# Routing moved into the attention steps of a gated cross-attention block with a mixture of experts

## Chip, cores and metric

The kernel runs on one core of a Trainium2 chip. The metric is the device time of one execution in microseconds (us). Three timed runs of the kernel before are 759.17, 760.97 and 762.27 us; their median is 760.97.

## The reference, cut to what matters

There are 64 sequences of 64 tokens with 128 features (4096 tokens), in float32. All learned scales and biases are drawn at random, so none can be left out.

```python
x = x + tanh(g_xattn) * cross_attention(layernorm(x), ctx)   # 16 heads of 64, q and k layer-normed per head, softmax, Wu, bu
h = layernorm(x)
probs = softmax(h @ Wg)                        # 8 experts
vals, idx = top_k(probs, 2); weights = vals / (sum(vals) + 1e-9)
routed = sum over the two chosen e of weights[e] * (silu(h @ W1[e] + b1[e]) @ W2[e] + b2[e])   # 128 -> 512 -> 128
shared = silu(h @ Ws1 + bs1) @ Ws2 + bs2
x = x + tanh(g_ffn) * (routed + 0.1 * shared)
```

## The kernel before

The tokens are 32 tiles of 128 (two sequences each). Every engine has its own queue, run in the order in which the code is written; semaphores carry the dependences. PE is the matmul engine, DVE, ACT and POOL are the vector, scalar and GpSimd engines, SP issues DMAs. Large projections are made of three float32r passes on a high and a low part of each operand: ACT copies the high part, POOL or DVE subtracts it from the value for the low part.

**Attention.** A Python loop over steps s writes out, for each engine, what it does for a tile and its neighbours: projections of q and k for tiles s+1 and s+2, normalisation, transposes, scores of tile s, softmax (DVE maxima and subtraction, ACT exponential, DVE row sums and reciprocals, then POOL's `normalise_rows`, one multiplication over 128x1024), the attention output of tile s-1 and the output projection of tile s-2. The calls in each engine's `step(s)` are its order. In the same steps ACT and POOL split a 160-column slice of the expert weights W1 (`expert_weights`). At s == 1 ACT issues the loads of all expert weights (`load_experts`).

**Routing and shared expert.** After attention, `groups` runs over eight groups of four tiles; groups 0, 1, 6 and 7 are written out, the others are a loop. A group computes the shared expert's hidden layer and result for group g, logits for group g+1, and the choice of experts for g: softmax over 8, `max` and `max_index` per tile, one-hot masks, running counts in bfloat16, and a matmul with a triangular matrix that gives each token its rank. POOL then scatters the normalised rows into the `routed` table in device memory, one region for each expert, one indirect DMA per tile and choice. DVE adds the shared result to the residual (`shared_out`). At the end DVE makes a schedule of 39 row tiles of 256 rows, and the ends of regions are filled with padding rows.

**Routed tiles.** For each of the 39 tiles SP loads 256 rows (four buffers), PE transposes them, ACT and DVE split them, DVE copies the W1 parts of the expert, PE does hidden layer and result, and POOL scatters the result by the row's index (`xs_ix`) into `results`. The last stage reads both results of each token and adds them with their weights.

Of the kernel before, what the change touches and what calls it, by code (L numbers as in the profile page):

```python
# [13 lines left out]
P = 128  # L14
# [9 lines left out]
GT = 4  # L24
# [3 lines left out]
ROW = D + 1  # L28
# [10 lines left out]
def flamingo_block(nc, x, xT, ctxT, g_xattn, g_ffn, wqT, wkT, wvT, wuT, bu, qn_w, qn_b, kn_w, kn_b,  # L39
                   wg, w1, b1, w2, b2, ws1, bs1, ws2, bs2, out):  # L40

    with ExitStack() as stack:
# [15 lines left out]
        xc_hi = sb("xc_hi", [P, 2, 2, P], F32R)  # L58
        xc_lo = sb("xc_lo", [P, 2, 2, P], F32R)
# [17 lines left out]
        spo = sb("spo", [P, 2 * E * (D + 1)])  # L77
# [14 lines left out]
        mv = sb("mv", [P, 2, 2])  # L92
# [5 lines left out]
        w1_raw = sb("w1_raw", [P, NX, FF])  # L98
# [8 lines left out]
        rows = late[:, 0:2 * 2 * GT * ROW].rearrange("p (u c j n) -> p u c j n", u=2, c=2, j=GT)  # L107
        o = 2 * 2 * GT * ROW
        router = {}
        for name, width in (("lg", GT * E), ("gm", GT), ("gs", GT), ("gtop", GT * 8), ("gidf", GT * 2), ("gw", GT * 2),  # L110
                            ("oh", 2 * GT * E), ("rank", GT * E), ("hit", 2 * GT * E), ("slotf", 2 * GT)):
            router[name] = late[:, o:o + width]
            o += width
        assert o <= 3 * INNER
        gp = router["lg"].rearrange("p (j e) -> p j e", j=GT)
        gm, gs = router["gm"], router["gs"]
        gtop = router["gtop"].rearrange("p (j e) -> p j e", j=GT)
        gidf = router["gidf"].rearrange("p (j e) -> p j e", j=GT)
        gw = router["gw"].rearrange("p (j e) -> p j e", j=GT)
        oh = router["oh"].rearrange("p (c j e) -> p c j e", c=2, j=GT)  # L120
        rank = router["rank"].rearrange("p (j e) -> p j e", j=GT)
        hit = router["hit"].rearrange("p (c j e) -> p c j e", c=2, j=GT)
        slotf = router["slotf"].rearrange("p (c j) -> p c j", c=2)
        y8 = prob[:, 0:4, :, :].rearrange("p a b n -> p (a b n)")
        spare_hi, spare_lo = (w[:, :, :].rearrange("p a n -> p (a n)") for w in (w_hi, w_lo))
        gT = spare_lo[:, 0:2 * GN].rearrange("p (u n) -> p u n", u=2)
        gT_hi, gT_lo = gT[:, 0, :], gT[:, 1, :]
        act = wide[:, 0:2, :].rearrange("p a n -> p (a n)").rearrange("p (c n) -> p c n", c=CH)
# [4 lines left out]
        normed = wide[:, 2:4, :].rearrange("p a (j n) -> p a j n", n=D)[:, :, 0:GT, :]  # L133
        gidx = sb("gidx", [P, GT, 8], U32)
        chosen = sb("chosen", [P, 2, GT, E], BF16)
# [86 lines left out]
        def steps(step):  # L222
            for s in range(-5, TILES + 5):
                step(s)
# [1043 lines left out]
```

## Time and profile before

| | us |
|---|---|
| median of three runs | 760.97 |
| profiled execution, own time | 757.15 |
| its span, first to last instruction | 755.1 |
| PE busy | 612.6 (81%) |
| DVE busy | 480.6 (64%) |
| ACT busy | 456.8 (60%) |
| POOL busy | 363.6 (48%) |

The profile is of one execution; the time around its span is 2.05 us. A matmul in float32 shows as two instructions. Busy times overlap between engines; a queue named with a q (ACTq, SPq) is the time an engine spends on issuing a DMA or on registers. "issue" and "remote" name idle time whose cause the profile does not show.

### The profile page before, as it was taken

Reading aid. Unit: us, or ns where it says so; the run is one execution under the profiler, and the core shown is the slowest. Engines: PE = TensorE matmul, PEld = TensorE weight load, DVE = VectorE, ACT = ScalarE, POOL = GpSimd, SP = SyncE. Lnnn points to the kernel's source line nnn. Section 1 sums busy time; section 2 is a strip of 40 time slices with the busy share of each in tenths; the row PEclk is TensorE's granted clock in tenths of the full one; section 3 lists DMA queues with packets and bytes.
Section 4 is the critical chain, followed back from the end, with each engine's and each line's share of the span. In section 5 each row is a group of like instructions: output and inputs, shape, how many; then the busy total and the mean of one; then the engine's idle time right before and its main releaser. Section 6 shows DMA issues by size and latency. Waiting matters only on the chain.

```text
span 755.1 us, 21530 instructions
## 1 busy us (share of the span) xinstructions
PE 612.6 (81%) x7702; PEld 531.3 (70%) x7702; DVE 480.6 (64%) x1191; ACT 456.8 (60%) x967; POOL 363.6 (48%) x713
## 2 busy tenths in 40 slices
PE   3709999999999999999998588777734989898950
PEld 1508787877878778787787476766634989898940
DVE  5626888888888888888887356645552444444417
ACT  4517888888888888888887235333402545454515
POOL 3423556555555555555654315554461545454540
PEclk9869999999999999999999668887865999999985
DMA  7180000000100000000000040111033212222218
GB/s 245 41 263 18 2 30 3 3 30 2 31 2 3 30 3 30 2 3 3 2 2 3 1 79 32 40 35 35 29 79 63 76 59 76 67 72 71 72 42 327
DMA packets 30038, 37.90 MB, mean 50 GB/s; under 512 B 4993, under 2 KB 20625, under 8 KB 29809
## 3 DMA queue, kind: packets, MB, share of 16 engines
q1 hardware_dynamic: 20800, 21.42, 9.5%
q0 software_dynamic: 4720, 9.89, 4.0%
q10 hardware_dynamic: 4416, 5.25, 2.6%
q8 instruction: 62, 1.02, 0.6%
q14 instruction: 40, 0.32, 0.1%
HBM read 23.13 MB, written 13.42 MB: 48 GB/s over the span
## 4 chain that ended last, share of the span: by engine, by line
PE 56%; ACT 11%; DVE 11%; issue 8%; another core or an unknown queue 5%; DMA 3%; ACTq 3%; POOL 2%; SPq 0%; DVEq 0%; POOLq 0%
PE ps L1039 8%; PE ps L1221 8%; PE ps L1012 6%; PE ps L1014 5%; PE ps L1013 5%; PE ps L1065 4%; PE ps L1048 4%; ACT prob L419 4%; PE ps L1080 4%; PE ps L1207 3%; PE ps L1209 3%; ACT qk_T L404 3%; PE ps L1208 2%; ACTq L348 2%
## 5 line engine op out<-in xcount | busy, mean ns | idle before, releaser
L663 POOL DMA_INDIRECT results<-spo,xs_ix x78 | 75.2, 964 | 87.2 <-DVE spo L986 72.2
L740 DVE TENSOR_REDUCE ss<-wide 128x16 f32<-128x1024 f32 x64 | 78.1, 1220 | 53.0 <-ACT wide L380 45.9
L509 ACT ACTIVATE qk_T<-ps,b_cols 128x256 f32<-128x256 f32 x156 | 61.9, 474 | 75.9 <-PE ps L1209 69.9
L404 ACT ACTIVATE qk_T<-ps,lnw 128x512 f32<-128x512 f32 x128 | 96.7, 787 | 15.4 <-issue 14.1
L1039 PE MATMUL ps<-ident,wide 128*128 128x128 f32 x512 | 76.3, 282 | 32.3 <-ACT qk_T L404 31.5
L1039 PEld LDWEIGHTS ps<-ident,wide 128*128 128x128 f32 x512 | 57.9, 142 | 58.8 <-ACT qk_T L404 44.5
L1012 PE MATMUL ps<-w_hi,xc_hi 128*128 128x512 f32 x192 | 91.7, 477 | 7.3 <-DVE w_lo L683 3.8
L646 POOL DMA_INDIRECT routed<-w_raw,slot x64 | 62.2, 972 | 70.9 <-issue 53.3
L747 DVE TENSOR_TENSOR wide<-ps,rstd 128x512 f32<-128x512 f32 x128 | 81.7, 680 | 3.7 <-POOL rstd L598 3.3
L380 ACT ACTIVATE wide<-ps 128x512 f32<-128x512 f32 x128 | 77.3, 606 | 5.0 <-PE ps L1014 5.0
L1014 PE MATMUL ps<-w_hi,xc_lo 128*128 128x512 f32 x192 | 77.2, 402 | 0.0
L1013 PE MATMUL ps<-w_lo,xc_hi 128*128 128x512 f32 x192 | 76.9, 401 | 0.0
L1221 PE MATMUL ps<-w_sb,qk_T 128*128 x624 | 76.9, 277 | 0.0
L1221 PEld LDWEIGHTS ps<-w_sb,qk_T 128*128 128x128 f32 x624 | 73.8, 194 | 0.0
L1094 PEld LDWEIGHTS ps<-wu_sb,spo 128*128 128x128 f32 x512 | 63.5, 196 | 5.3 <-ACT spo L434 2.8
L1094 PE MATMUL ps<-wu_sb,spo 128*128 128x128 f32 x512 | 64.2, 280 | 2.5 <-ACT spo L434 2.5
L604 POOL TENSOR_TENSOR prob<-prob,rinv 128x1024 f32<-128x1024 f32 x32 | 61.0, 1905 | 9.2 <-DVE rinv L776 9.2
L1207 PE MATMUL ps<-w_lo,w_hi 128*128 128x256 f32 x156 | 49.0, 314 | 8.5 <-DVE w_lo L957 8.4
L769 DVE TENSOR_REDUCE sm<-prob 128x16 f32<-128x1024 f32 x32 | 39.1, 1221 | 17.5 <-ACT prob L419 17.5
L755 DVE TENSOR_REDUCE mx<-ps 128x8 f32<-128x512 f32 x64 | 41.2, 686 | 12.5 <-PE ps L1065 12.4
L957 DVE TENSOR_TENSOR w_lo<-ps,w_lo 128x256 fp32r<-128x256 f32 x39 | 16.6, 425 | 49.3 <-ACT w_lo L500 38.8
L1012 PEld LDWEIGHTS ps<-w_hi,xc_hi 128*128 128x128 f32 x192 | 37.2, 194 | 15.2 <-DVE w_lo L683 5.8
(175 smaller groups left out, 1419.7 us busy)
## 6 DMA issues: line engine op xcount, KB each, us to landing
v_sb<-routed SPq DMA_DIRECT2D x39, 129.0 KB
xc_in<-in_x SPq DMA_DIRECT2D x8, 256.0 KB, 2.9
xc_in<-in_ctx SPq DMA_DIRECT2D x8, 256.0 KB, 3.2
w_raw<-in_L_ffn_W ACTq DMA_DIRECT2D x1, 2048.0 KB, 9.7
wide<-results SPq DMA_DIRECT2D x4, 512.0 KB, 4.9
w_raw<-results SPq DMA_DIRECT2D x4, 512.0 KB, 8.0
out_x<-x_res SPq DMA_DIRECT2D x8, 256.0 KB, 3.9
x_res<-in_x SPq DMA_DIRECT2D x1, 1792.0 KB, 8.5
```

The lines of the kernel that those rows point to most:

```text
L380: nc.scalar.activation(sq[:, n, j * 512:j * 512 + 512], ps[2 * n + j][:, :], ACT.Square, scale=HD ** -0.5).then_inc(sq_ready[n][j], 1)
L404: nc.scalar.activation(qk_T[:, n, 4 * j:4 * j + 4, :].rearrange("p a n -> p (a n)"), ps[6 + j][:, :], ACT.Identity, bias=lnw[:, 2 * n + 1: ...
L663: gp_.indirect_dma_start(out=results[:, :], out_offset=bass.IndirectOffsetOnAxis(ap=xs_ix[:, b4, a:a + 1], axis=0), in_=yb[:, b4, a, :], i ...
L740: nc.vector.tensor_reduce(ss[:, n, :], sq[:, n, :].rearrange("p (h d) -> p h d", h=HEADS), AX.X, ALU.add).then_inc(ss_ready[n], 1)
L747: nc.vector.tensor_tensor(qk_n[:, n, j * 512:(j + 1) * 512].rearrange("p (h d) -> p h d", h=8), ps[2 * n + j][:, :].rearrange("p (h d) -> ...
L1012: nc.tensor.matmul(out_bank, xc_hi[:, t % 2, src, :], w_hi[:, w, cols[j]], start=True, stop=False)
L1013: nc.tensor.matmul(out_bank, xc_hi[:, t % 2, src, :], w_lo[:, w, cols[j]], start=False, stop=False)
L1014: return nc.tensor.matmul(out_bank, xc_lo[:, t % 2, src, :], w_hi[:, w, cols[j]], start=False, stop=True)
L1039: last = nc.tensor.transpose(ps[6 + j][:, a * P:(a + 1) * P], qk_n[:, n, c0:c0 + P], ident[:, :])
L1094: last = nc.tensor.matmul(ps[7][:, 0:D], o_T[:, p, :, :].rearrange("p b n -> p (b n)"), wu_sb[:, p, :], start=(p == 0), stop=(p == PAIRS - 1))
L1207: nc.tensor.matmul(h, w_hi_c, xs_hi[:, n % 2, :], start=True, stop=False)
L1221: last_ = nc.tensor.matmul(ps[4 + n % 2][:, a * D:(a + 1) * D], hT[:, n % 2, c, a * P:(a + 1) * P], w2e[:, c, :], start=(c == 0), stop=(c ...
```

## The change

- Routing is worked into the attention steps. Tile s-3 is normalised, transposed and multiplied by Wg (float32, no split) inside step s. The choice is made for batches of eight tiles, in eight pieces, one per step from step 12 on (`batch_at`, `route`), straight behind the row reciprocals on DVE. It finds the best expert by maximum, equality and a factor that prefers the first of ties, and then the second; counts are per batch. The last of the four batches is done after attention.
- The scatters are two per step from step 20 on POOL (`SCATTER_LAG`); the rest follow the steps. Rows are scattered from one table `rows_all` of all tiles; both choices send the same row, which carries the token's index and its first expert, so that the reader can tell first from second choice.
- Order within `step` is new on all engines; token parts have four buffers in place of two (`XD`). POOL splits W1's low part (the rest) a step after ACT's high part. W1 is handled in 27 parts of 176 or 160 columns.
- Expert loads are issued by SP, W1 one expert at a time into two buffers. The bias loads and all padding writes are on SP too; DVE makes the padding in place of POOL.
- The shared expert is written out, with two buffers for its inputs, activations and sums; its first two hidden layers stand among the last attention steps.
- Rows have 130 columns, and the 256 rows of a routed tile lie two per partition.

```diff
 def step(s):                                   # PE
-    project_qk(0, 1, s + 1)
-    transpose_qk(0, 1, s, before_q)
-    project_v(1, s)
...
-    transpose_probabilities(0, s - 1, before_p)
-    transpose_probabilities(1, s - 1, before_p)
-    scores(s)
-    attend(s - 1)
+    if s == TILES:
+        transpose_tokens(0)
+        transpose_tokens(1)
+        shared_hidden(0)
+    transpose_probabilities(0, s - 1, before_p)
+    transpose_probabilities(1, s - 1, before_p)
+    scores(s)
+    attend(s - 1)
+    project_qk(0, 1, s + 2)
+    transpose_qk(0, 0, s + 1, before_q)
+    logits(s - 4)
+    route_ranks(s, 12)
+    transpose_qk(0, 1, s + 1, before_q)
+    project_qk(1, 1, s + 2)
+    project_v(0, s + 1)
+    transpose_normed(s - 3)
+    project_out(s - 1)
+    transpose_qk(1, 0, s + 1, before_k)
+    project_qk(1, 0, s + 2)
+    transpose_qk(1, 1, s + 1, before_k)
+    project_v(1, s + 1)
+    project_qk(0, 0, s + 3)
+    if s == TILES:
+        transpose_tokens(2)
+    if s == TILES + 1:
+        shared_hidden(1)
 def step(s):                                   # DVE
+    sum_squares(0, s + 1)
+    scale(1, 0, s)
+    row_sums(s - 1)
+    row_inverses(s - 1)
+    route(s, 12)
     residual(s - 2)
-    token_statistics(s + 3)
     scale(0, 0, s + 1)
-    scale(0, 1, s + 1)
     sum_squares(1, s + 1)
+    scale(0, 1, s + 1)
+    normalise(s - 3)
+    token_statistics(s + 3)
     second_statistics(s - 2)
     maximum(1, s)
     maximum(0, s)
     less_maximum_of(1, s)
+    scale(1, 1, s + 1)
     less_maximum_of(0, s)
-    sum_squares(0, s + 2)
-    scale(1, 1, s + 1)
-    scale(1, 0, s + 1)
-    row_sums(s)
-    row_inverses(s)
+    route_ranks(s, 12)
+    keep_logits(s - 4)
 def step(s):                                   # POOL
+    scatter(s - SCATTER_LAG)
+    variance(1, s)
+    newton_step(1, s)
+    output_bias(s - 2)
+    token_eps(s + 1)
+    expert_weights(s - 1)
+    low_part(s + 3)
+    second_rstd(s - 3)
+    variance(0, s + 1)
+    newton_step(0, s + 1)
+    normalise_rows(s - 1)
+def route(s, lag):                             # DVE, one piece per step
+    b, at = batch_at(s, lag)
...
+    if at == 0:
+        less_highest(b)
+    if at == 1:
+        expert_probabilities(b)
+        highest(0, gp)
+        ties(0, gp)
+    if at == 2:
+        chosen(0)
+        without_first()
+        highest(1, rest)
+    if at == 3:
+        ties(1, rest)
+        chosen(1)
+    if at == 4:
+        count(b)
+    if at == 5:
+        fill_ranks(b)
+        name_first(b)
+    if at == 6:
+        place(b)
+    if at == 7:
+        weigh(b)
+def scatter(t):                                # POOL
+    if has(t):
+        gp_.wait_ge(f_slot, t // BT + 1)
+        for c in range(2):
+            gp_.indirect_dma_start(out=routed[:, :], out_offset=bass.IndirectOffsetOnAxis(ap=slot[:, t // BT, c, t % BT:t % BT + 1], axis=0),
+                                   in_=rows_all[:, t, :], in_offset=None).then_inc(f_sent, 16)
 # PE, after the steps
+shared_result(0)
+for g in range(1, GROUPS):
+    if g + 2 < GROUPS:
+        transpose_tokens(g + 2)
+    if g + 1 < GROUPS:
+        shared_hidden(g + 1)
+    if g == 1:
+        ranks(NB - 1)
+    shared_result(g)
 # routed tiles
-sp.dma_start(xs_in[:, b4, :, :], routed[bass.ds(row, RT), :].rearrange("(a p) n -> p a n", p=P)).then_inc(r_in[b4], 16)
+sp.dma_start(xs_in[:, b4, :, :], routed[bass.ds(row, RT), :].rearrange("(p a) n -> p a n", p=P)).then_inc(r_in[b4], 16)
-nc.vector.tensor_copy(xs_ix[:, b4, :], xs_in[:, b4, :, D].bitcast(I32)).then_inc(r_ix, 1)
+nc.vector.scalar_tensor_tensor(xs_ix[:, b4, :], xs_in[:, b4, :, D + 1], sched[:, 0, n:n + 1], xs_in[:, b4, :, D],
+                               ALU.not_equal, ALU.add).then_inc(r_ix, 1)
```

On DVE, the order after the steps is: the last batch's choice with `lo_part(2)` in it, `shared_out(0)`, `lo_part(3)`, the last slots, `make_padding`, `shared_out(1)`, `lo_part(4)`, the schedule of 22 short linked instructions, and then the other sums and low parts.

## Rows read from the trace of the kernel before

**Rows 1.** Stretches: length, busy (count) PE PEld DVE ACT POOL, clock, DMA share, GB/s.
```profile
61.30:412.40 351.10, 334.81 (x5567) 278.26 (x5566) 287.63 (x501) 298.62 (x620) 198.20 (x496) 1.00 0.03 10
440.60:577.80 137.20, 91.33 (x561) 79.81 (x560) 74.94 (x393) 44.78 (x63) 62.20 (x64) 0.76 0.19 46
577.80:735.00 157.20, 142.62 (x1168) 139.93 (x1166) 64.34 (x190) 72.38 (x194) 75.20 (x78) 0.97 0.21 65
```

**Rows 2.** Chain that ended last: start us, us, what (L1065 is the scores).
```profile
61.34 1.09 PE ps L1065 x64
...
391.75 1.09 PE ps L1065 x64
...
412.47 1.14 PE ps L1065 x64
...
429.82 0.36 DVE x_res L723
...
569.31 3.86 DMA routed<-w_raw,slot
```

**Rows 3.** Timeline of ACT at start-up: start us, us, what, idle before.
```profile
42.28 12.17 ACTq L348 DMA_DIRECT2D w_sb<-in_L_ffn_Ws  x1
...
55.46 0.78 ACT L404 ACTIVATE qk_T<-ps,lnw 128x512 f32<-128x512 f32 x1 [14.11 <-issue]
```

**Rows 4.** Timeline inside an attention step, PE and POOL.
```profile
199.93 1.09 PE L1039 MATMUL ps<-ident,wide 128*128 128x128 f32 x8 [0.48 <-ACT qk_T L404]
...
200.36 1.91 POOL L604 TENSOR_TENSOR prob<-prob,rinv 128x1024 f32<-128x1024 f32 x1
```

**Rows 5.** Groups by line, 440 to 560 us: busy us, mean ns, idle before.
```profile
L646 POOL DMA_INDIRECT routed<-w_raw,slot x56 | 54.5, 973 | 65.1 <-issue 47.5 <-DVE slot L913 17.6
...
L873 DVE TENSOR_TENSOR w_raw<-iot,w_raw 128x32 f32<-128x32 f32 x16 | 2.3, 191 | 0.0
...
L911 DVE TENSOR_REDUCE w_raw<-w_raw 128x8 f32<-128x64 f32 x8 | 1.8, 220 | 0.3
```

**Rows 6.** Lines L804 and L683: ns minimum/median/maximum, first and last start us.
```profile
L804 DVE TENSOR_SCALAR wide<-x_res,mv,rstd x32: 328/346/3556, 430.6 to 522.0; 128x128 f32<-128x128 f32 x16, 128x128 f32 x16
...
L683 DVE TENSOR_TENSOR w_lo<-w_raw,w_hi x4: 692/693/860, 10.2 to 15.7; 128x512 fp32r<-128x512 f32 x4
```

**Rows 7.** Timeline at start-up, POOL and DVE.
```profile
16.15 2.57 POOL L621 TENSOR_TENSOR w_lo<-w_raw,w_hi 128x512 fp32r<-128x512 f32 x2 [4.46 <-ACT w_hi L373]
...
16.27 1.30 DVE L780 TENSOR_SCALAR tgbu<-bu_b,tg 128x128 f32<-128x128 f32 x1
```

**Rows 8.** Timeline after attention, POOL's padding fill.
```profile
432.04 1.82 POOL L650 MEMSET spo<- 128x2064 f32 x1
```

**Rows 9.** Timeline from the last scatters to the first routed tile.
```profile
555.79 0.96 POOL L646 DMA_INDIRECT routed<-w_raw,slot  x1 [0.30 <-issue]
...
559.54 0.17 DVE L931 CAST cnt_i<-run 128x8 int32<-128x8 f32 x1
...
565.15 0.20 DVE L952 CAST sched_i<-sched 128x78 int32<-128x78 f32 x1
...
567.16 0.43 DVE L971 CAST w_hi<-w_hi 128x512 fp32r x1 [0.42 <-issue]
...
577.84 0.58 PE L1207 MATMUL ps<-w_lo,w_hi 128*128 128x256 f32 x1
```

**Rows 10.** Timeline of PE in group 1: hidden layer, transposes, result.
```profile
452.29 0.48 PE L1156 MATMUL ps<-w_lo,w_hi 128*128 128x512 f32 x1
...
455.19 0.60 PE L1141 MATMUL ps<-ident,wide 128*128 128x128 f32 x4
...
456.81 3.81 PE L1168 MATMUL ps<-w_sb,wide 128*128 128x128 f32 x32 [1.03 <-ACT wide L480]
```

**Rows 11.** Waits in total, 440 to 560 us: us, times, longest us.
```profile
ACT w_raw L475 <- DVE w_raw L842: 68.8, 8, 9.9
POOL routed L646 <- issue: 47.5, 55, 5.8
```

More of the change, by code:

```diff
@@ L254, in eps_of, with batch_at @@
             return eps_q[:, t % 4:t % 4 + 1] if n == 0 else eps[:, 1, 0:1]
[L256 to L264 removed]
+        def batch_at(s, lag):
+            b, at = divmod(s - lag, BT)
+            return (b, at) if 0 <= b < NB - 1 else (None, 0)
         def r_slot(n):
@@ new lines, in _ @@
+            load_expert(0)
+            load_expert(1)
+            load_experts()
+            for s in range(TILES):
+                c, at = divmod(s, CK)
+                if at == 0 and c + 2 < TILES // CK:
+                    sp.wait_ge(xlo_ready, CK * (c + 1))
+                    load_tokens(c + 2)
+                e, part = divmod(s - W1_FIRST, len(W1_PARTS))
+                if part == len(W1_PARTS) - 1 and 2 <= e + 2 < NX:
+                    load_expert(e + 2)
+            sp.dma_start(b1_cols[:, :], b1).then_inc(bias_in, 16)
@@ L466, in _ @@
+                if s == TILES:
+                    shared_silu(0)
             steps(step)
[L468 to L483 removed]
@@ L485, in _ @@
[L485 to L494 removed]
+            hi_part(2)
+            expert_exponentials(NB - 1)
@@ new lines, in route_ranks, with transpose_tokens @@
+            def route_ranks(s, lag):
+                b, at = batch_at(s, lag)
+                if b is not None and at == RANKS_AT:
+                    ranks(b)
+            def transpose_tokens(g):
+                pe.wait_ge(norm_ready, GT * g + GT)
+                if g == 0:
+                    pe.wait_ge(sub_ready[0], TILES)
+                else:
+                    pe.wait_ge(f_lo, g)
+                for j in range(GT):
+                    last = nc.tensor.transpose(ps[4][:, j * P:(j + 1) * P], rows_all[:, GT * g + j, 0:D], ident[:, :])
+                last.then_inc(f_t, 1)
@@ new lines, in shared_result @@
+            def shared_result(g):
+                pe.wait_ge(act_ready, CH * (g + 1))
+                if g >= 1:
+                    pe.wait_ge(f_x2, 2 * g - 1)
+                else:
+                    pe.wait_ge(o_ready[0], TILES)
+                for j in range(GT):
+                    for c in range(CH):
+                        last = nc.tensor.matmul(ps[6][:, j * D:(j + 1) * D], act[:, g % 2, c, j * P:(j + 1) * P], w2_sb[:, E, c, :],
+                                                start=(c == 0), stop=(c == CH - 1))
+                last.then_inc(fy_done, 1)
```

651 lines of the change are left out of this document (325 added, 326 removed).

## Prediction, made before the changed kernel was run

> **What bounds the kernel now.** I read the table of stretches first, cut where the work changes [rows 1]. Up to 61.3 us is start-up. From 61.3 to 412.4 us the attention steps run: PE is busy 334.8 of 351.1 us at full clock, DVE 287.6, ACT 298.6, POOL 198.2. The score matmuls in the chain give the period: from 61.34 (token tile 1) to 391.75 (tile 29) is 28 periods of 11.80 us [rows 2]. Per step that is PE 11.25 busy and 0.55 idle, DVE 9.67, ACT 10.04, POOL 6.66. So PE bounds a step, with only 0.55 us in which it stands. From 440.6 to 577.8 us the routing and the shared expert take 137.2 us, of which PE is busy 91.3 at clock 0.76 and no engine is full: this stage is a ring of waits. From 577.8 us the 39 routed tiles run, PE busy 142.6 of 157.2; then the last sums. The change aims at the third stage and pays in the second.
>
> **Start-up.** The old load_experts sat on ACT's queue. The issue for the small Ws2 load took 12.17 us there, because the large W2 load ahead of it had to be taken in first, and ACT's next operation came after 14.11 us of idleness [rows 3]. In the new kernel these loads are on SP, where only loads needed several steps later stand behind them; W1 comes expert by expert. W1's two first parts are ahead of W2, and tokens for tiles 8 on are first needed at step 4. I take the whole 14.1, and 1.0 more because PE came back at the lower clock. **-15.** If SP's loads came late instead, the cover would be gone and up to all 15 lost.
>
> **The attention steps, PE.** Per tile a transpose of the normalised rows and a logits matmul are added, each two passes. A transpose pass is one 128-column instruction that PE issues every 0.14 us (1.09 us for eight [rows 4]); so 0.27 for the transpose, and, as its weight load is the same, 0.25 for the logits. Two rank matmuls per eight tiles are under 0.1. Sum 0.52 on 11.25: 11.8 if all gaps close, 12.3 if the present 0.55 stays. The order is rewritten so that each projection stands between a copy and the matmul that needs it; I take 12.1, thus +0.3 a step. For the eleven periods before routing starts (score tiles 1 to 12): **+3**.
>
> **The attention steps, DVE.** From step 12 each step carries an eighth of a batch's choice. The pieces have 34 instructions for 8 tiles, most of 64 elements. The nearest rows are 0.22 us for a reduction over 64 and 0.19 for a two-input operation on 32 [rows 5], and the wait on DVE's own last instruction adds about 0.02: 34 times 0.21 is 7.1 us per batch, 0.9 a step. The normalising of a tile is 0.33 (the minimum in [rows 6]) and the logits copy 0.17. That makes 9.67 + 0.9 + 0.33 + 0.17 = 11.1 us, still under PE.
>
> But the piece stands straight behind the reciprocal of the row sums, and that is what releases POOL's 1.9 us multiplication over the probabilities [rows 4]. What such a pair does is seen at start-up: the 128x128 tensor_scalar that takes 0.33 elsewhere took 1.30 when it began at 16.27, 0.12 us after POOL began the first of its two 1.28 us subtractions; of 32 normalisations one took 3.56 us, while POOL cleared the padding; and a two-input subtraction with both inputs in SBUF took 0.86 against 0.69 when a POOL subtraction was under way [rows 6 to 8]. So an operation that needs both SBUF inputs can be held until POOL is done. All eight pieces contain two-input operations on SBUF; the first short instruction slips in, the rest would stand up to 1.7 us. Bounds: 0 and 1.7 a step; I take 1.5, since each of the three shows a hold where POOL overlapped, though the last only a part of it. Then DVE needs 12.6 a step, and in its fixed order nothing else can fill the hole: residual, two scalings, a reduction, two statistics stand behind the piece, and PE's next score-dependent work waits for the maxima behind those. I take 12.7, 0.9 over the present, for the 17 periods from tile 12 to tile 29: +15.3. The last two periods are now 20.7 us together [rows 2] and bound by latency; I take 23 for them. **+18** together.
>
> The Trainium skill, page "SBUF — State Buffer", section "Who interferes with whom", says that a DVE instruction with two SBUF inputs and a GpSimd instruction that reads SBUF exclude each other for the whole instruction, and that a reduction never does. By that rule the hold is about 1.8 us and the period 12.9 to 13.0, 4 us more in all; without any hold it would be 12.1, 10 us less. The long tensor_scalar rows agree with it in kind [rows 6, 7]; the 0.86 us row is shorter than a full hold.
>
> **ACT and POOL in the steps.** ACT gains a 128x128 copy, some 0.3, and one exponential in eight: 10.4 of 12.1. Its W1 piece is 176 wide, not 160. POOL gains from step 20 two scatters per step, each 0.97 busy [rows 5] and, at its closest, 0.30 apart [rows 9]: 2.5, so 9.2 of 12.7. Ahead of the reciprocal roots on POOL's queue they delay the key scaling; that scaling is needed only after the next scores and POOL has 3.5 us to spare, so nothing. The single-tile expert loads are covered by three steps of lead, and SP's waits for POOL's subtraction hold up only loads that are wanted later.
>
> **From the last scores to the routed tiles.** Now: 412.47 to 577.84, 165.4 us [rows 2, 9]. The last tile's residual begins 17.3 us after its scores began [rows 2]; attend and output ran at the low clock there. In the new kernel the shared expert's first hidden layers are put among them, so PE stays busy; at the upper clock this piece loses about 3, giving 14.5. Statistics, root, normalising, transpose, copy, logits and copy for tile 31 are seven short links of 0.2 to 0.6, about 3.5. So the choice for the last eight tiles can start 18 us after the last scores began.
>
> After that, PE has eight shared results, six hidden layers, five sets of four transposes. A hidden layer took 2.9 us at full clock (452.29 until 455.2) and a result 3.6 (the 3.81 row less the overlap of its last matmul) [rows 10]; transposes 0.6: 28.8 + 17.4 + 3.0 = 49.2. DVE meanwhile has the last choice (34 x 0.21 = 7.1), the padding it takes from POOL (a fill of 2064 columns is 1.82 us on POOL [rows 8]; I take that and 1.6 for the shorter one on DVE too), the schedule (559.54 to 565.35, 5.8 us [rows 9]) and the sums of each group (1.4 and 0.7). Since result g waits for sum g-1, PE stands about 2, 1 and 1.2 us behind these three lumps: 4.4. That replaces the ring that now costs about 15 us per group: there ACT waits 68.8 us in eight waits for the logits' maximum [rows 11], and the exponential, hidden activations and result stand in series behind. Scatters: 32 of them are left, 1.26 each, 40 us, plus 3.9 us to the last landing [rows 2]; their last slots are ready 12 us after the choice starts. They end near 43 of the 54 us: hidden, with 11 us to spare. The eight padding transfers on SP start once the counts are known, some 15 us into this phase, and have the rest of it.
>
> Then the last sum (1.4), DVE's four W1 copies of 0.43 with 0.4 before each pair [rows 9] (2.5) and the first low part (0.4): 4.3 us. Total 18 + 49.2 + 4.4 + 4.3 = 76, against 165.4: **-89.5**.
>
> **Routed tiles.** Rows of 520 B, two per partition, halve the packets of the loads, but PE is the bound there at 91% of the stretch, and the loads wait in four buffers: 0. The index operation now compares the expert, 0.05 more on a DVE busy 64 of 157 us: 0. At the beginning PE ran at the low clock until about 582; after dense work it need not: **-2**.
>
> Sum: -15 + 3 + 18 - 89.5 - 2 = -85.5. The profiled execution has 757.15 us of its own, 2 over its span, and lies 3.8 under the median of 760.97. So 671.7 in its terms, 675.5 in those of the median: I say **674**.
>
> **Rivals.** (a) No hold, PE bounds all steps. For it: DVE's tiny inputs may not need the port for long. Against: [rows 7]. Step 11.85 to 12.1: total 652 to 664. Chance 0.22. The forecast itself, steps of 12.4 to 13.2, has 0.5 and its own range 664 to 688.
> (b) The shared expert stays stop-and-go: PE falls to the low clock (it is 0.76 there now [rows 1]) or each result waits for a sum; then a group costs 9.5 instead of 7.1, over seven groups +17, total about 691. Against: its inputs are ready one group ahead. Chance 0.16.
> (c) The gain is cut because scatters, not PE, release the routed tiles: at 2.0 us each rather than 1.26, 24 us more, less 11 to spare: 687. For: they share POOL and DMA with padding; against: the 56 of now have a mean of 0.97 [rows 5]. Chance 0.08.
> (d) Slower: POOL's queue. If a scatter inside a step waits as long as its longest idle gap now (5.8 us, the longest of 55 [rows 11]), POOL gets past the reciprocal roots late, scaling follows and every step with scatters grows. It decides from 85.5/16 = 5.3 us a step; at 5.8 on top of the forecast it gives 674 + 93 = 767. Against: slots are written a step or more before. Chance 0.02. The last 0.02 is for about no change.
>
> **Numbers.** From (a) through (b): 652 to 696 leaves out about 2 in 10 at the two ends. What a measurement here can tell from no change is about 0.5%, 3.8 us. Faster 0.96, within 0.02, slower 0.02.
>
> **What would show it.** Score matmuls of neighbouring tiles 12.1 apart up to tile 12 and 12.7 beyond it; in heavy steps a two-input DVE instruction of the piece 1 to 1.8 us long, ending with POOL's multiplication; no idle of 14 us in ACT; PE's gap before the first routed matmul under 5 us; the shared phase near 7.1 us per group at a clock near 1. Wrong it would be above all if the heavy steps are far from 12.7, or if long instruction waits turn up in the code of the groups, which is now written out.

## The result: 714.6 us, faster, but by 47 us and not by 87

The changed kernel took 714.63 us (median of four runs, 712.04 to 716.72) beside 761.43 for the kernel before: a ratio of 0.9371, 95% interval 0.9333 to 0.9408. Faster, as predicted, but outside the range of 652 to 696. The profiled execution took 712.84 us, its span is 710.8.

One thing has to be said before any number below is read. The experiments ran in five batches on chips of the same kind, each batch beside the kernel before. In two batches the kernel before took 712.8 and 712.5 us, in three 750.5, 762.2 and 760.5, and the traces of the latter hold pauses of ACT and DVE that those of the former lack. The comparison above is of the second sort. So each ratio below is to the kernel before in the same batch, and microseconds are compared within one batch or stage by stage.

The chain that ended last of the changed kernel (start us, us, what; L1137 is the scores, L1319 the first routed matmul) answers to [rows 2]:

```profile
43.83 1.09 PE ps L1137 x64
...
170.02 1.14 PE ps L1137 x64
...
399.17 1.14 PE ps L1137 x64
...
425.98 1.14 PE ps L1137 x64
...
456.85 16.46 another core or an unknown queue
...
488.27 10.83 another core or an unknown queue
...
534.65 0.58 PE ps L1319
```

From it, with the kernel before in the same stretches:

| stretch | predicted | before, us | after, us | difference |
|---|---|---|---|---|
| up to the scores of tile 1 | -15 | 61.34 | 43.83 | -17.5 |
| tile 1 to 12, eleven light periods | +3 | 130.4 | 126.2 | -4.2 |
| tile 12 to 29, seventeen heavy periods | +15.3 | 200.0 | 229.2 | +29.1 |
| tile 29 to 31 | +2.3 | 20.7 | 26.8 | +6.1 |
| last scores to first routed matmul | -89.5 | 165.4 | 108.7 | -56.7 |
| routed tiles and last sums | -2 | 177.3 | 176.2 | -1.1 |
| sum | -85.5 | 755.1 | 710.8 | -44.3 |

(The prediction rounds its third and fourth term to 18 together. In the kernel before the scores of tile 12 start at 191.71. Differences are of unrounded times.) Three terms are off by more than 5 us: the light steps by 7, to the good, the heavy steps by 14 and the stage behind the last scores by 33, both to the bad. Stretches of the changed kernel (length, busy (count) of PE PEld DVE ACT POOL, clock, DMA share, GB/s), against [rows 1]:

```profile
43.80:170.00 126.20, 123.41 (x2076) 107.74 (x2075) 111.50 (x208) 113.58 (x240) 73.33 (x183) 1.00 0.07 21
170.00:399.20 229.20, 198.58 (x3222) 170.08 (x3225) 205.29 (x397) 178.89 (x376) 139.26 (x310) 0.98 0.07 20
426.00:534.60 108.60, 73.17 (x638) 65.45 (x638) 45.10 (x130) 35.86 (x59) 40.94 (x44) 0.87 0.14 48
534.60:690.00 155.40, 141.77 (x1166) 139.50 (x1166) 65.82 (x190) 72.04 (x193) 75.39 (x78) 0.97 0.20 65
```

In the light steps PE is busy 123.4 of 126.2 us: it bounds them, at 11.35 a step between tiles 3 and 11. In the heavy steps PE is busy 198.6 of 229.2 and DVE 205.3: PE stands 1.8 us a step. In the third stretch no engine is busy for more than 73 of 108.6 us.

**A heavy step.** Heavy periods run from 11.15 to 15.16 us, 13.48 on average. The timeline of the changed kernel behind the reciprocals in one of the longest (15.07 us), POOL, DVE and PE one after the other (start us, us, engine, line, tiles, idle before):

```profile
284.83 1.90 POOL L613 TENSOR_TENSOR prob<-prob,rinv 128x1024 f32<-128x1024 f32 x1
...
284.74 0.20 DVE L809 RECIPROCAL w_raw<-w_raw 128x8 f32<-128x8 f32 x1
284.98 1.83 DVE L810 TENSOR_TENSOR w_raw<-w_raw 128x64 f32<-128x64 f32 x1
286.85 0.22 DVE L813 TENSOR_REDUCE w_raw<-w_raw 128x8 f32<-128x64 f32 x1
287.10 0.23 DVE L816 TENSOR_TENSOR w_raw<-w_raw 128x64 f32<-128x64 f32 x1
287.36 0.35 DVE L721 SCALAR_TENSOR_TENSOR x_res<-ps,tg,x_res 128x128 f32<-128x128 f32 x1
...
287.77 0.66 PE L1111 MATMUL ps<-ident,wide 128*128 128x128 f32 x4 [2.16 <-DVE x_res L721]
...
289.02 0.63 PE L1079 MATMUL ps<-w_hi,xc_hi 128*128 128x512 f32 x1
289.45 0.63 PE L1080 MATMUL ps<-w_lo,xc_hi 128*128 128x512 f32 x1
```

The hold is there as forecast: a multiplication over 64 columns starts 0.15 us after POOL's, takes 1.83 us and ends 0.08 after it; its neighbour of the same form takes 0.23. What the prediction did not follow is the line behind the piece. The residual (L721) frees the PSUM bank (PSUM is the memory that PE writes to) into which PE puts the next key transposes, so PE stands 2.16 us, and after that its float32r matmuls come 0.43 apart in place of 0.23. The granted clock of that stretch:

```profile
283.00:287.70 4.70, 2.61 (x21) 2.12 (x19) 4.49 (x10) 3.08 (x9) 3.56 (x7) 1.00 0.02 3
287.70:291.60 3.90, 3.83 (x17) 3.26 (x18) 3.35 (x9) 2.12 (x5) 1.59 (x3) 0.65 0.10 34
```

PE waits for the residual in 15 of the 17 heavy steps, 1.4 to 2.3 us each. The clock fell only behind some of these waits: it is 0.89 over each of three periods of 15.1 to 15.2 us (one wait of 2.2 us in each) and 1.00 from 170 to 223, 238 to 277, 292 to 330 and 330 to 384 us, where the waits are 1.4 to 2.3 us.

**The stage behind the last scores.** ACT, DVE, POOL and SP in the same timeline:

```profile
454.43 2.42 ACT L443 ACTIVATE wide<-ps,bs_sb 128x512 f32<-128x512 f32 x4
...
468.45 0.75 DVE L949 SCALAR_TENSOR_TENSOR prob<-ps,tg,x_res 128x512 f32<-128x512 f32 x1 [8.60 <-remote]
...
470.07 0.96 POOL L631 DMA_INDIRECT routed<-rows_all,slot  x1 [0.30 <-issue]
...
473.33 0.60 ACT L465 ACTIVATE w_lo<-ps 128x512 fp32r<-128x512 f32 x1 [16.48 <-remote]
...
476.19 0.96 POOL L631 DMA_INDIRECT routed<-rows_all,slot  x1 [5.16 <-DVE slot L860]
...
484.73 16.90 SPq L313 DMA_DIRECT2D routed<-spo  x7
...
495.45 0.96 POOL L631 DMA_INDIRECT routed<-rows_all,slot  x1 [0.30 <-issue]
...
499.12 0.75 DVE L949 SCALAR_TENSOR_TENSOR prob<-ps,tg,x_res 128x512 f32<-128x512 f32 x1 [10.68 <-remote]
...
499.18 0.60 ACT L465 ACTIVATE w_lo<-ps 128x512 fp32r<-128x512 f32 x1 [19.36 <-remote]
```

ACT waits 16.48 us before a copy whose transposes PE had done at 455.4; DVE waits 8.60 before a sum whose matmuls were done at 455.0. Neither waits for anything the profile shows ("remote"). Beside them runs POOL's stream of scatters, one every 1.26 us, 18 from 448.4 until 471.0 and then 16 until 496.4. ACT goes on 2.3 and 2.8 us after the end of a stream; DVE goes on 2.7 us after the end of the second, but 2.6 us before the end of the first. PE has such idle time too ("issue" in place of "remote"). Beside the second stream SP needs 16.9 us to issue seven padding DMAs.

### The profile page after: what moved, and what is told of

It reads as the page before. It is cut to its first block, busy times and chain, and to the rows that moved or that the text cites. A ratio compares the mean times of both kernels' runs of the same rounds, so it can differ in the third digit from the quotient of the medians.

```text
span 710.8 us, 21126 instructions
## 1 busy us (share of the span) xinstructions
PE 585.2 (82%) x7614; PEld 519.6 (73%) x7614; DVE 490.7 (69%) x1045; ACT 453.8 (64%) x982; POOL 362.4 (51%) x706
## 4 chain that ended last, share of the span: by engine, by line
PE 57%; DVE 22%; issue 8%; another core or an unknown queue 4%; ACT 4%; DMA 3%; POOL 1%; SPq 0%; ACTq 0%; DVEq 0%; POOLq 0%
PE ps L1333 8%; PE ps L1111 5%; PE ps L1137 5%; PE ps L1079 4%; PE ps L1120 4%; PE ps L1081 4%; PE ps L1080 4%; PE ps L1167 4%; PE ps L1319 3%; DVE sm L767 3%; PE ps L1321 3%; PE ps L1235 3%; DVE wide L745 3%; PE ps L1152 3%
## 5 line engine op out<-in xcount | busy, mean ns | idle before, releaser
L1111 PE MATMUL ps<-ident,wide 128*128 128x128 f32 x512 | 80.3, 283 | 35.6 <-DVE x_res L721 34.2
L1111 PEld LDWEIGHTS ps<-ident,wide 128*128 128x128 f32 x512 | 60.3, 148 | 53.5 <-DVE x_res L721 42.2
L1079 PE MATMUL ps<-w_hi,xc_hi 128*128 128x512 f32 x192 | 89.9, 468 | 8.1 <-DVE wide L745 3.9
L745 DVE TENSOR_TENSOR wide<-ps,rstd 128x512 f32<-128x512 f32 x128 | 87.1, 681 | 4.4 <-POOL rstd L607 4.4
L1081 PE MATMUL ps<-w_hi,xc_lo 128*128 128x512 f32 x192 | 78.9, 411 | 0.0
L631 POOL DMA_INDIRECT routed<-rows_all,slot x64 | 64.1, 1002 | 22.3 <-issue 16.7
L1167 PEld LDWEIGHTS ps<-wu_sb,spo 128*128 128x128 f32 x512 | 61.3, 196 | 3.3 <-issue 0.4
L753 DVE TENSOR_REDUCE mx<-ps 128x8 f32<-128x512 f32 x64 | 41.2, 686 | 27.9 <-PE ps L1137 27.9
L1319 PE MATMUL ps<-w_lo,w_hi 128*128 128x256 f32 x156 | 49.0, 314 | 10.5 <-DVE w_lo L1023 10.5
L1235 PE MATMUL ps<-w_sb,wide 128*128 128x128 f32 x256 | 34.5, 297 | 26.2 <-DVE prob L949 25.8
L1235 PEld LDWEIGHTS ps<-w_sb,wide 128*128 128x128 f32 x256 | 33.2, 211 | 27.9 <-issue 27.6
L598 POOL TENSOR_TENSOR newton<-root 128x16 f32<-128x16 f32 x64 | 13.9, 217 | 77.1 <-ACT root L389 77.1
```

Source lines behind the costliest of these rows:

```text
L745: nc.vector.tensor_tensor(qk_n[:, n, j * 512:(j + 1) * 512].rearrange("p (h d) -> p h d", h=8), ps[2 * n + j][:, :].rearrange("p (h d) -> ...
L1079: nc.tensor.matmul(out_bank, xc_hi[:, t % XD, src, :], w_hi[:, w, cols[j]], start=True, stop=False)
L1081: return nc.tensor.matmul(out_bank, xc_lo[:, t % XD, src, :], w_hi[:, w, cols[j]], start=False, stop=True)
L1111: last = nc.tensor.transpose(ps[6 + j][:, a * P:(a + 1) * P], qk_n[:, n, c0:c0 + P], ident[:, :])
L1167: last = nc.tensor.matmul(ps[7][:, 0:D], o_T[:, p, :, :].rearrange("p b n -> p (b n)"), wu_sb[:, p, :], start=(p == 0), stop=(p == PAIRS - 1))
L1235: last = nc.tensor.matmul(ps[6][:, j * D:(j + 1) * D], act[:, g % 2, c, j * P:(j + 1) * P], w2_sb[:, E, c, :], start=(c == 0), stop=(c == ...
```

## The experiments

They were made with two questions: what lengthens the heavy steps, and what the pauses are.

**1. The piece behind the residual.** `route(s, 12)` one line down on DVE.

```diff
-                route(s, 12)
                 residual(s - 2)
+                route(s, 12)
```

> DVE's piece of the choice stands one instruction later, behind the residual. Theory A (the residual's lateness is what PE waits for, 2.2 us in a step, because the second key transposes need the bank that it reads; the low clock after it costs more): the hold of 1.5 to 1.85 us on a two-input operation stays, PE's wait before the second key transposes goes, the steps from tile 12 on fall from 13.5 to 12.3 to 12.7 us, the whole by 15 to 23 us, to 692 to 700. Rival B (DVE is simply full with the hold in it, wherever it stands): the steps stay above 13.2 and the time within 4 us of 714.6.

659.92 us, ratio 0.9283 (0.9241 to 0.9325). Heavy periods 12.87 in place of 13.48, the last two 23.4 in place of 26.8, light ones unchanged. Against the changed kernel in the same kind of batch (671.9, experiment 5) it is 12 us, and its last scores begin 12.9 us earlier than there. The mechanism is as expected, the gain smaller than the 15 to 23 us. The eight periods of a batch, one for each piece from tile 12 on, were 12.77, 13.53, 14.09, 13.02, 11.96, 15.15, 12.90 and 13.12 us in the changed kernel and are 12.09, 12.86, 13.23, 12.98, 12.40, 13.14, 12.93 and 13.13 now. So the gain is 0.7 to 0.9 us in three of them and 2.0 in the one with the low clock. In the fourth, seventh and eighth there is none, although PE no longer waits for the residual there: it now waits 1.6 to 1.8 us for DVE's scaling L745, which has come to stand behind the piece (1.59 at 205.78, 1.55 at 244.25, 1.75 at 257.37). The residual is shown as a term; the pauses, missing here, have nothing to do with it.

**2. The piece before the maxima**, after `second_statistics(s - 2)`, when POOL's multiplication is over.

> The piece stands behind the second statistics, ahead of the maxima, when POOL's multiplication over the probabilities is long done. If POOL's multiplication is what holds the two-input operations, they fall to 0.23 us, and DVE has 1.6 us less in a step: steps of 11.8 to 12.3, the whole 690 to 700. If the long operations come from something else, they stay 1.5 us and more, and the maxima, now behind them, make the steps 13 or longer (712 or more).

637.15 us, ratio 0.8965 (0.8927 to 0.9003): 35 us below the changed kernel without pauses (671.9, below). Heavy periods 11.84, the last scores 31.4 us earlier. L810 took 0.25 us in the median of its four executions.

**3. The scatters last.** POOL waits for the last sum of the shared expert before the 32 scatters that follow the steps (`wait_ge(f_x2, 2 * GROUPS)`).

> POOL begins the 32 scatters that follow the steps only when the last shared sum is done. Theory A (DVE and ACT stood 8.6 to 19.4 us with nothing to wait for because their next code comes slowly while a close row of scatters runs): those idle times go, the eight shared results follow each other in 7 us or less, the last sum falls from 531 to about 504, the scatters then take 41 us and 4 to land, and the routed tiles start near 552; the whole is 728 to 735. Rival B (the pauses belong to the written-out code of the groups and come anyway): the last sum stays at 531, the routed tiles start near 578 and the whole is 755 to 762.

714.48 us, ratio 1.0026 (1.0003 to 1.005), in a batch without pauses: 43 us over the changed kernel there. So the scatters are hidden in the changed kernel of that kind of batch, and bare they cost their 32 x 1.26 and a landing.

**4. The scatters drained**, in bursts of four.

```diff
 for t in range(LAST_STEP - SCATTER_LAG + 1, TILES):
+    if t % 2 == 0:
+        gp_.wait_ge(f_sent, 16 * 2 * t)
     scatter(t)
```

> After the steps POOL waits before every second tile (every fourth scatter) until all its scatters have landed. Theory A: in each pause of 2 to 3 us the waiting code gets through, so no idle time of ACT or DVE is over 7 us, the last shared sum comes at 505 to 518, the scatters end at 510 to 515, and the whole is 692 to 705. Rival B (pauses in the code that have nothing to do with the scatters): the idle times of 16.5 and 19.4 us on ACT stay and the time is 714 to 722.

672.82 us, ratio 0.9436 (0.9406 to 0.9466). I read this as a gain of 40 us from draining. The next run took that back.

**5 and 6. The changed kernel itself, and with one fill more on DVE.** All four variants lacked the pauses, which no single mechanism explained.

> The changed kernel itself, submitted like every experiment. Two ways to read the three variants that lost ACT's and DVE's pauses: (T) the pauses come from how the scatter stream meets the shared groups in time, which each variant shifted; (P) they belong to something that is set for a whole execution of a program, and any other program would lose them. Both expect 712 to 715 here, a ratio within 0.5% of 1, and the two pauses of ACT before L465. If it comes out at 670 to 680 instead, neither is right: then the pauses come from the place among the runs and not from the program, and the comparisons of the first four experiments were unfair by 35 to 40 us.

> The changed kernel with one more instruction on DVE, a fill of 64 elements at step 6, some 0.1 us, long before any scatter. T: nothing moves in time, so the pauses stay, 712 to 716. P: it is another program, the pauses go and the time is 670 to 680.

671.9 us beside 712.46, ratio 0.9428 (0.9379 to 0.9477), and with the extra fill 671.76 (0.9378 to 0.9477). The unchanged kernel ran 43 us faster than in its first measurement, and in the same ratio to the kernel before, since that was faster too. Draining had gained nothing. Both readings that I had written down were wrong. The chain and stretches of this run, the changed kernel without pauses:

```profile
423.56 1.50 PE ps L1137 x64
...
504.13 0.58 PE ps L1319
```

```profile
169.40:397.00 227.60, 198.17 (x3222) 169.72 (x3225) 205.05 (x397) 178.96 (x376) 139.19 (x310) 0.98 0.07 20
423.50:504.10 80.60, 68.24 (x639) 61.57 (x638) 44.85 (x130) 36.02 (x58) 41.41 (x44) 0.97 0.19 64
```

The heavy steps are as long as before (17 periods of 13.39). The stage behind the last scores is 80.6 us, for which 76 was predicted, at a clock of 0.97 in place of 0.87. The routed tiles with the last sums take 165.5 in place of 176.1. So the 41.2 us between the two spans are 28.1 in that stage, 10.6 in the routed tiles and 2.4 in attention.

**7. Piece before the maxima, and drained.**

> The piece before the maxima (as in the second experiment, 637.15) and the scatters after the steps in bursts of four with a wait for their landings (as in the fourth). With the piece before the maxima no pause was left, so there is nothing for the bursts to gain; the waits of 2.3 us, eight of them, put the last scatter at about 468 instead of 454, still before the schedule at 472 or just at it. T and P both: 637 to 641. If it is below 630, the two gains add and the pauses are only hidden in the second experiment.

640.96 us, ratio 0.8981 (0.8941 to 0.9022), no pauses in the batch: as expected, nothing to gain from draining.

**8. The expert loads back on ACT's queue** (Wg, W2, Ws2, bias at step 1; W1 stays on SP), in the kernel of experiment 2.

> The piece before the maxima, with the loads of Wg, W2, Ws2 and the bias put back on ACT's queue at step 1; W1 stays on SP expert by expert. Compared with 637.15 for the same without this. If the start-up gain of 17.5 us is ACT's queue being blocked by an issue behind the large W2 load, ACT idles 10 to 14 us there and the time is 648 to 652. Rival: the gain came from W1 being loaded expert by expert, so that W2 is alone on the queue and no issue is held up: then 637 to 640.

645.56 us, ratio 0.9048 (0.9007 to 0.9088), 8.4 over 637.15. The scores of tile 1 start at 49.30 in place of 43.59. ACT's timeline of this run:

```profile
39.32 5.37 ACTq L457 DMA_DIRECT2D w_sb<-in_L_ffn_Ws  x1
...
45.70 0.60 ACT L366 ACTIVATE wide<-ps 128x512 f32<-128x512 f32 x1 [7.13 <-issue]
```

The issue behind the large W2 load takes 5.37 us, not the 12.17 of [rows 3]. So 5.7 of the 17.5 us come from leaving ACT's queue and, by difference, the other 12 from W1 no longer being loaded in one piece ahead of W2 and from the rest of the new start; these were not tried apart. The time lies between what the two expectations gave: the prediction had blamed the queue alone, the rival the size of W1 alone.

**9. The kernel before, unchanged.**

> The kernel before the change, submitted like every experiment; it was measured at 761.43 us as the kernel before. The unchanged changed kernel came out at 671.9 us in this way instead of 712.5, with every pause of unknown cause gone. If that belongs to the way a kernel is submitted, this one loses its own: six before the sums of the shared expert and one before the ranks (39.8 us of DVE's idle time), and four of ACT in the routed tiles worth about 3 us each. Not all of the 40 was on the path, so 715 to 735. If only the changed kernel was affected: 755 to 765.

751.48 beside 750.46 us, ratio 0.9998 (0.9958 to 1.0039), with its pauses. The batch had them for all its kernels. The changed kernel itself was not in it; its nearest stand-in is experiment 11 (709.57 us, ratio 0.9473), whose edit made no difference beside the changed kernel (experiment 15). So experiments 10 and 12 are compared with 709.57 in the same batch.

**10. POOL after the piece.** The direct test of the hold: POOL's multiplication waits until DVE's piece is done.

```diff
 gp_.wait_ge(rinv_ready, t + 1)
+b, at = batch_at(t + 1, 12)
+if b is not None:
+    gp_.wait_ge(f_step, 29 * b + (1, 6, 11, 15, 16, 21, 24, 29)[at])
```

> The changed kernel, with POOL's multiplication over the probabilities held until DVE's piece is done, so that no operation of the piece can be held by it. To be compared with 671.9 for the unchanged kernel. If the hold by POOL is what makes the piece long (1.8 us for a two-input operation), the residual behind it starts about 1 us earlier in 24 steps, while the multiplication itself starts about 0.8 later and has room: steps of 12.5 to 12.9 in place of 13.4, 650 to 662. Rival: the piece is long by its own linked instructions, and the multiplication only comes later: 672 to 685.

687.36 us, ratio 0.9152 (0.9087 to 0.9217), 22 us below experiment 11 in the same batch, although a wait was added; its last scores begin 19.8 us earlier than there. The timeline of one step, and the line by itself (ns minimum/median/maximum):

```profile
175.42 0.22 DVE L813 TENSOR_TENSOR w_raw<-w_raw 128x64 f32<-128x64 f32 x1
...
175.93 0.22 DVE L819 TENSOR_TENSOR w_raw<-w_raw 128x64 f32<-128x64 f32 x1
...
176.30 1.90 POOL L616 TENSOR_TENSOR prob<-prob,rinv 128x1024 f32<-128x1024 f32 x1 [1.00 <-DVE w_raw L819]
```

```profile
L813 DVE TENSOR_TENSOR w_raw<-w_raw x4: 224/224/226, 175.4 to 433.3; 128x64 f32<-128x64 f32 x4
```

In the changed kernel the same instruction reads:

```profile
L810 DVE TENSOR_TENSOR w_raw<-w_raw x4: 226/1834/1837, 177.8 to 453.8; 128x64 f32<-128x64 f32 x4
```

Heavy periods are 12.43, against 13.44 in experiment 11: 11.5 to 12.5 up to tile 20, where the scatters begin, and 12.3 to 13.2 behind. The hold is shown, and with it most of the difference between the 13.39 of the changed kernel and the 11.84 of experiment 2.

**11 and 15. One row per partition.** The load of a routed tile as "(a p)" in place of "(p a)", twice the packets.

> The changed kernel, with the 256 rows of a routed tile read one per partition and half (partition p gets rows p and p + 128) in place of two neighbours, so that a load is 256 packets of 520 B in place of 128 of 1040 B. The result is the same sum over the same rows. Priced at nothing: PE bounds the routed tiles and the loads are four tiles ahead, so 670 to 674 beside 671.9. Rival: loads and scatters share the DMA engines (0.2 busy there), and a later landing stops PE: 5 us or more longer.

> One row per partition and half again, now beside the changed kernel itself: the same within 3 us if the loads are covered, 5 us or more slower if not.

709.57 us (ratio 0.9473, 0.94 to 0.9546) in a batch without the changed kernel, and 712.62 (0.9341, 0.9306 to 0.9375) beside 713.89 for it: no difference. The 0.9473 of the first lies above the 0.937 of the changed kernel in other batches with pauses, so ratios of different batches agree to about 1% only. Two rows per partition bought nothing, as priced.

**12. The piece at the end of DVE's step.**

> The piece as the last thing of DVE's step, behind the subtraction of the maxima (the one of the counts before the maxima, since PE's rank matmuls of the same step need it). Compared with 637.15 for the piece before the maxima. There it delays the maxima, the exponential and the row sums behind it by 0.8 us, while the multiplication has ended long before. At the end it delays only the next sum of squares and the row sums, for which ACT's exponential is still at work: if the exponential's latency is cover, 632 to 636; if DVE's order is full at that place too, 637 to 642.

685.95 us, ratio 0.9146 (0.9083 to 0.921), 24 us below experiment 11, heavy periods 12.37 against 11.84 before the maxima: up to tile 19 as short, afterwards 12.3 to 13.2. Both expectations failed (12.37 a step is half a microsecond over the place before the maxima). Why the steps with scatters suffer here, and in experiment 10, was not followed up.

**13, 14 and 16. Changed kernel, kernel before and experiment 2 in one batch.**

> The changed kernel unchanged once more. The kernel before, run beside each call, took 712.8, 712.5 and 750.5 us in three calls, the last two on one chip, and the changed one 671.9 beside 712.5 but 714.6 beside 761.4: so ACT's and DVE's pauses come or stay away for all kernels of a call together. With the kernel before near 712: 670 to 674 and no pause. With it at 750: 700 to 707 and the pauses. The ratio to the kernel before is 0.934 to 0.945 either way. If the ratio is outside that, the pauses are not common to a call.

> The kernel before, for its trace. With pauses: as in the first trace, 750 to 760. Without them (some 712): the shared stage, from the last scores to the first routed matmul, takes 125 to 132 us in place of 165.4, the routed tiles 165 in place of 177, and the attention steps are unchanged. Rival: the time is lost everywhere, in the attention steps as well, and then the last scores begin 10 us or more before 412.

> The piece before the maxima once more, beside the changed kernel itself. The steps are untouched by the pauses, so it is 33 to 36 us faster than the changed kernel in the same call, whether the pauses are there or not: a ratio to the kernel before of 0.89 to 0.90. If it has no pauses where the changed kernel has them, 60 us or more faster, then the place of the piece matters for the pauses after all.

The kernel before took 762.2 us, the changed one 713.89, ratio 0.9366 (0.9331 to 0.9402); experiment 2's kernel 680.54, ratio 0.8929 (0.8888 to 0.897). All three with pauses, in ratios that agree with those of the batches without. So the pauses go with the batch, not with the kernel. Run 14 drew a batch with pauses, so there is no trace of the kernel before without them, and where its 49 us between 712.5 and 761.4 lie is not shown. The waits of the kernel before for causes unknown, in the trace of run 14 behind 400 us (total, times, longest):

```profile
DVE prob L826 <- remote: 31.6, 6, 6.8
...
DVE w_raw L903 <- remote: 7.5, 1, 7.5
```

**17. Drained, in a batch with pauses** (the kernel before 760.5).

> The changed kernel with the scatters after the steps in bursts of four, each burst drained before the next. Its first run was in a call without pauses and could not show what it was made for. If the kernel before takes about 760 here (pauses): if it is the length of the unbroken stream that starves ACT and DVE, the two long pauses before L465 go, some 20 to 28 us, ratio to the kernel before 0.90 to 0.915; if the pauses come with any scatters, 0.93 to 0.945 as for the changed kernel (0.937). If the kernel before takes about 712, it is 0.944 again and tells nothing new.

692.45 us, ratio 0.91 (0.9041 to 0.9159), against 0.9366 for the changed kernel in another batch with pauses. The two long pauses of ACT are gone, and those of DVE. Waits of this run and of the changed kernel from the last scores to the routed tiles:

```profile
DVE prob L951 <- PE ps L1237: 20.3, 5, 4.9
ACT w_lo L465 <- PE ps L1212: 19.6, 6, 5.1
POOL routed L631 <- DMA routed<-rows_all,slot: 15.6, 8, 3.5
```

```profile
ACT w_lo L465 <- remote: 35.8, 2, 19.4
...
DVE prob L949 <- remote: 19.3, 2, 10.7
```

**18. Scatters last, in the same batch.**

> The changed kernel with all 32 scatters after the steps held back until the shared expert's last sum. With pauses in the call (the kernel before near 760): the shared groups then run without a scatter beside them; if the pauses need the scatters, ACT and DVE have no idle time of unknown cause in these groups, the last sum comes at about 500 as in the call without pauses, and the time is 725 to 735 (the 40 us of scatters bare, the pauses of the routed tiles stay), a ratio of 0.955 to 0.965. If the pauses stay without scatters, 755 or more. In a call without pauses 714 again.

734.33 us, ratio 0.9646 (0.9603 to 0.9689). Its waits beside the shared groups name no unknown cause; the stretches (columns as above) are the groups and the bare scatters:

```profile
426.50:500.00 73.50, 64.34 (x599) 57.31 (x598) 39.72 (x120) 37.10 (x59) 11.87 (x16) 0.98 0.10 36
500.00:560.00 60.00, 10.93 (x72) 10.21 (x72) 6.03 (x12) 2.46 (x7) 30.64 (x32) 0.58 0.14 45
```

So where the long pauses of the shared stage occur, they need POOL's unbroken stream: without it, or with it broken up, the stage takes 127.7 and 85.0 us, against 123.5 and 80.7 for the same kernels in a batch without pauses, where the changed kernel goes from 80.6 to 108.7. That does not hold for the routed tiles. From the first routed matmul to the end these two kernels take 178.1 and 179.1 us with pauses and 164.1 and 164.8 without, so some 14 us stay in a stage in which POOL's scatters come in pairs.

## Why the prediction was wrong

**The stage behind the last scores: the term failed, by 33 us.** The step is the sum "Total 18 + 49.2 + 4.4 + 4.3 = 76". In a batch without pauses it measures 80.6, so the work was sized to 5 us. The other 28 are the pauses beside the two streams of scatters. (Its 4.4 is 4.2 by its own summands, 2, 1 and 1.2.) The prediction counted the scatters only as work of POOL that ends in time ("hidden, with 11 us to spare"), which experiment 3 bears out, and never asked what a long row of them does beside other engines. The trace of before had the answer: six pauses of DVE before a sum and one before the ranks, some 40 us in all, each ending 1 to 2 us after a burst of eight scatters. I read them as part of the ring of waits and removed them with it. The sentence on "long instruction waits in the code of the groups" named a place, not a cause, and gave it no price. Rival (c) had the scatters as cause, by their length; that was not it. For the same reason the forecast of the gain had the wrong base: beside the kernel before without pauses (712.46 us) the changed kernel is 40.6 us faster, and the -89.5 was taken from a stage of the kernel before that holds these 40 us of DVE's pauses.

**The heavy steps: mis-sized, +35.2 for +17.6 from tile 12 to the last scores.** The step is "Then DVE needs 12.6 a step ... I take 12.7". The hold itself was right, about 1.6 us where 1.5 was taken, and 1.8 by the rule of the Trainium skill (page "SBUF — State Buffer", section "Who interferes with whom"); experiment 10 agrees with the rule, since the same operation is 0.22 when POOL comes after it. The price was taken from DVE's queue alone. But the residual behind the piece frees a bank that PE needs, so the hold was passed on to PE, which stood 1.4 to 2.3 us in 15 of 17 steps and went on at the lower clock in some: 13.48 a step. Moving the piece behind the residual gave 12.87, near the 12.7 that DVE's sum says. So of the 29.1 us of the seventeen steps about 10 come from the residual's place (17 times 0.61). I had written that the residual stands behind the piece, without asking who waits for it.

**Light steps: the term +3 measured -4.2.** They are 11.35 a step, not 12.1. The prediction added 0.52 of new work to 11.25 of busy time ("11.8 if all gaps close, 12.3 if the present 0.55 stays"), and both numbers were too large. The new work, with the groups behind it, in a light step of the changed kernel:

```profile
138.14 0.29 PE L1191 MATMUL ps<-wg_raw,row_T 128*128 128x8 f32 x2
138.28 0.63 PE L1111 MATMUL ps<-ident,wide 128*128 128x128 f32 x4
...
140.17 0.27 PE L1180 MATMUL ps<-ident,rows_all 128*128 128x128 f32 x1
140.28 1.95 PE L1167 MATMUL ps<-wu_sb,spo 128*128 128x128 f32 x16
```

The group behind starts 0.14 us after the logits' two instructions and 0.11 after the transpose, which is one instruction and not two: 0.25. And a pass counts as busy for 0.40 us, while the next one can start after 0.23. In the kernel before two passes of a step have nothing behind them for their whole length, one of them this:

```profile
154.94 0.40 PE L1014 MATMUL ps<-w_hi,xc_lo 128*128 128x512 f32 x1
155.34 1.06 PE L1048 MATMUL ps<-ident,prob 128*128 128x128 f32 x8
```

So 0.34 of its 11.25 is not work that PE has to do. 11.77 less the idle 0.48 and these 0.34, plus 0.25, is 11.20; the shortest light periods are 11.13 to 11.19.

**Start-up: -15 against -17.5**, right in size, half right in cause (experiment 8). **Routed tiles: -2 against -1.1**; row packets nothing, as said.

**Rivals.** (a), no hold, is excluded. (b), stop-and-go, is what the trace with pauses looks like, and not for the reason given: without them a group takes 6.8 us where 7.1 was forecast. (d) did not occur: the kernel is faster in every comparison. By luck the total without pauses, 671.9, is near the 674 that was forecast on a time with them; that is errors of opposite sign (heavy steps too long, light steps, start-up and routed tiles shorter) and no confirmation.

**What is best.** The piece before the maxima: 0.8965 and 0.8929 of the kernel before in the two kinds of batch, 4.9 and 4.7% below the changed kernel by these ratios. Drained scatters were 2.8% faster where there are pauses (0.91 over 0.9366) and cost 1 to 4 us where there are none (both comparisons are across batches); the two together were run only without pauses.

## What to carry to other kernels

When an operation is put into a full step, follow two threads from the place where it goes: which two-input operation on SBUF will now run beside POOL, and which bank or buffer the operation just behind it frees; the second cost 0.5 us of the 1.6 us a step that the place of the piece cost here (13.39, 12.87 and 11.84 a step). A long row of indirect DMAs that is "hidden" by its length may still cost other engines time, as it did in three of five batches here; idle gaps of unknown cause beside such a row are the sign, as long as it is open whether they belong to the measurement. And before a variant's gain is explained, run the unchanged kernel in the same batch.

## What the runs showed of the hardware

- In three of five batches ACT and DVE stood up to 19.4 us beside a stream of scatters, with what their semaphores wait for long done, and SP took 2.4 us for each of seven issues (1.1 without pauses); in two batches the same program did not. Two chips had a batch of either kind. The difference is 38 to 50 us for the kernel before and 43 for the changed one. Each timed run comes with a span, so all of them were recorded.
- In each of the 12 traces with pauses the landing times of the routed loads and result scatters are missing from the list of DMA issues, and in each of the 8 without they are there (2.0 to 2.1 and 2.2 us). The Trainium skill, page "NOTIFIC — Programmer's Manual", section "When the ring fills", says that a full queue of notification records, by its setting, drops the new record, overwrites the oldest or stalls the engine that writes it. Missing records beside standing engines would fit with that, if the traces are made of such records, and then the pauses would belong to the measurement; no run here shows it.
- Another candidate is instruction code that arrives late beside the scatters. The list of DMA queues shows the transfers of instructions, 63 and 39 packets on two queues with pauses and without alike. In the changed kernel's trace there is none between 453 and 484 us, and one pause of DVE and one of ACT end in that stretch (468.45 and 473.33). So a late transfer did not end these two; it was not tested further.
- The cause of the pauses stays open. What is shown is that they come with the batch, for all kernels in it, and that the long ones of the shared stage need the unbroken stream.
